# Dense input in the free rows of the pair chunks, five chunks in layer one, eight one-hot tables for all samples

## The reference

```python
e = jnp.stack([tbl_0[ids[:, 0]], ..., tbl_25[ids[:, 25]]], axis=1)      # 512 x 26 x 128
combined = jnp.concatenate([e, r_dense_x[:, None, :]], axis=1)          # 512 x 27 x 128
interact = jnp.einsum('bfd,bgd->bfg', combined, combined)
z = interact[:, _TRIU_I, _TRIU_J]                                       # 512 x 351
h = jnp.concatenate([z, r_dense_x], axis=1)                             # 512 x 479
h = jnp.maximum(h @ W_top1 + b_top1, 0.0)                               # 512
h = jnp.maximum(h @ W_top2 + b_top2, 0.0)                               # 256
y = h @ W_top3                                                          # 1
```

## Time and profile before

| | us |
|---|---|
| median of 3 runs (lowest, highest) | 120.97 (120.47, 121.06) |
| the profiled execution | 120.48 |
| its span | 118.7 |
| PE busy / DVE busy / POOL busy | 110.9 / 93.1 / 71.6 |

### The profile page before, as it was taken

One profiled execution on the slowest core, in us unless ns is written; L12 is line 12 of the kernel. 1 busy time (PEld: TensorE's weight loads), 2 busy tenths in 40 slices (PEclk: granted clock), 3 DMA queues, 4 the chain that ended last, 5 costly groups with the idle time before them and its releaser, 6 DMA issues.

```text
span 118.7 us, 2740 instructions
## 1 busy us (share of the span) xinstructions
PE 110.9 (93%) x794; PEld 88.0 (74%) x794; DVE 93.1 (78%) x379; ACT 50.6 (43%) x147; POOL 71.6 (60%) x80
## 2 busy tenths in 40 slices
PE   4999999999999999999989999799999996999990
PEld 4844454546454799759979898699998895998980
DVE  1699999999999998984999999940689992589312
ACT  5970640506050618930355871105686104586110
POOL 3477777777777776776777777776777750000000
PEclk9999999999999999999999999999999999999999
DMA  3999757454535125897321221221221220000000
GB/s 83 303 319 383 205 168 242 76 215 88 184 111 181 51 68 96 321 355 226 72 51 46 67 45 50 52 63 45 61 59 46 61 50 0 6 0 0 0 0 1
DMA packets 6543, 13.20 MB, mean 111 GB/s; under 512 B 2033, under 2 KB 3569, under 8 KB 6401
## 3 DMA queue, kind: packets, MB, share of 16 engines
q0 software_dynamic: 2336, 4.79, 15.1%
q1 hardware_dynamic: 3328, 5.50, 13.9%
q10 hardware_dynamic: 864, 2.75, 7.5%
HBM read 13.03 MB, written 0.00 MB: 110 GB/s over the span
## 4 chain that ended last, share of the span: by engine, by line
POOL 58%; issue 19%; PE 14%; DMA 5%; POOLq 1%; DVE 1%; ACT 0%; DVEq 0%
POOL rows L329 58%; PE gram_ps L625 6%; PE h_ps L660 3%; DMA idx<-in_ids_dram 3%; DMA rows<-in_tbl_dram,idx 2%; PE turn_ps L645 2%; PE h_ps L645 1%; POOLq L102 1%; PE gram_ps L645 1%; PE turn_ps L631 0%; DVE h L485 0%; DVE h_prod L487 0%; PE turn_ps L598 0%; ACT XT L374 0%; PE gram_ps L631 0%
## 5 line engine op out<-in xcount | busy, mean ns | idle before, releaser
L329 POOL DMA_INDIRECT rows<-in_tbl_dram,idx x73 | 70.5, 966 | 24.0 <-issue 22.0
L430 DVE COPY PAIRS<-gram_ps 27x60 f32<-27x60 f32 (+1 forms) x96 | 24.3, 253 | 11.6 <-PE gram_ps L625 10.2
L625 PE MATMUL gram_ps<-XT 128*123 128x80 f32 x256 | 28.5, 269 | 1.2 <-ACT XT L374 0.9
L625 PEld LDWEIGHTS gram_ps<-XT 128*123 128x123 f32 x256 | 27.9, 188 | 2.0 <-ACT XT L374 1.4
L374 ACT COPY PAIRS<-gram_ps 27x60 f32<-27x60 f32 (+1 forms) x96 | 23.3, 243 | 10.3 <-PE gram_ps L625 9.2
L374 ACT COPY XT<-turn_ps 128x512 f32<-128x512 f32 (+3 forms) x20 | 12.2, 619 | 34.3 <-PE turn_ps L598 18.2
L455 DVE CUSTOM_DVE_ANT_0 few_prod<-rows 128x128 f32<-128x128 f32 x84 | 20.6, 289 | 0.8
L513 DVE TENSOR_SCALAR onehot<-hot_ids,first_row 125x512 bf16<-125x512 int16 (+1 forms) x64 | 19.4, 374 | 2.4 <-DMA hot_ids<-in_hot_ids_dram 2.1
L645 PE MATMUL h_ps<-PAIRS,W1P 128*128 128x128 f32 x130 | 16.8, 276 | 0.2
L645 PEld LDWEIGHTS h_ps<-PAIRS,W1P 128*128 128x128 f32 x130 | 15.5, 192 | 0.5 <-ACT PAIRS L374 0.3
L588 PE MATMUL turn_ps<-onehot,hot_tab 125*128 125x512 bf16 (+3 forms) x56 | 11.7, 351 | 0.0
(11 more groups left out here) (49 smaller groups left out, 87.0 us busy)
## 6 DMA issues: line engine op xcount, KB each, us to landing
hot_tab<-in_hot_dram ACTq DMA_DIRECT2D x5, 512.0 KB, 3.6
rows<-in_tbl_dram SPq DMA_DIRECT2D x128, 0.5 KB
...
rows<-in_tbl_dram,idx POOLq DMA_INDIRECT x73, 2.9
...
```

The source lines that it names most:

```text
L329: pool.indirect_dma_start(rows[:, t, s, :], None, tables[f], bass.IndirectOffsetOnAxis(ap=idx[:, t, f:f + 1], axis=0)) \
L430: return nc.vector.tensor_copy(dst, src)
L625: last = nc.tensor.matmul(gram_ps[0:GRAM_ROWS, 2 * (i % 2) + q // fours, o:o + QUAD * NCOL], four.rearrange("d s f -> d (s f)")[:, 0:GRAM_ ...
```

## The change

- Slots are dealt anew (SLOT_FIELD, with ROW_SLOT from the order of the gathered rows to the slots): the first three gathered fields stand in slots 24 to 26. Rows 24 to 26 are no longer copied from gram's result (KEPT = 24 rows of a quadrant instead of 27; 120 weight columns). The three pairs among them join `few_pairs`: 24 dot products a tile, in goes of 8. With 8 free rows in each quadrant, all 24 fit in chunk 0, so `few` is one transpose and one add.
- The free rows of chunks 1 to 4 (4 quadrants x 8 rows x 4 chunks = 128) hold the dense input, loaded into PAIRS by four DMAs; W1D and its 16 matmuls go, layer one has five chunk matmuls a group. Only chunk 0 is zeroed by ACT.
- Table 25 joins HOT: prepared for all samples, tile 0 of it in the first phase and the rest behind the gram of tile 0 (as table 24 before); table 24 is now done for all samples in the first phase. `late_hot` and the seventh gather group go.
- The first ids load goes from ACT's queue to second place in SP's; the other ids loads are cut 1 + 6 tables instead of 2 + 5; x and its transpose come behind table 2. ACT places the dense input behind its fifth bank.
- The warm-up matmuls use a zeroed tile of their own instead of `ident`, and are 9 instead of 8.

```diff
-FEW = [(a, g) for g in range(FIRST) for a in range(g)]
+KEPT = 24
+APART = NVEC - KEPT
+FEW = [(a, g) for g in range(KEPT, NVEC) for a in range(KEPT, g)] + [(a, g) for g in range(FIRST) for a in range(g)]
...
-SPARE = SLOTS - NVEC
-FEW_PER_CHUNK = 4 * SPARE
-FEW_CHUNKS = -(-len(FEW) // FEW_PER_CHUNK)
-FEW_COLS = (FEW_CHUNKS - 1) * P + SLOTS
+PADDING = SLOTS - NVEC
+SPARE = SLOTS - KEPT
 FEW_PARTS = 3
 FEW_GO = len(FEW) // FEW_PARTS
 ALONE = 3
-assert len(FEW) == FEW_PARTS * FEW_GO and FEW_CHUNKS == 2 and len(FEW) - FEW_PER_CHUNK <= SPARE
-GRAM_ROWS = SLOTS * (QUAD - 1) + NVEC
+assert len(FEW) == FEW_PARTS * FEW_GO <= 4 * SPARE and D == 4 * SPARE * (PART_COLS - 1)
+GRAM_ROWS = SLOTS * (QUAD - 1) + KEPT
...
-WARM_UP = 8
+WARM_UP = 9
 RING = 3
-
-HOT = [1, 5, 7, 9, 12, 18, 24]
+DENSE_AFTER = 4
+
+HOT = [1, 5, 7, 9, 12, 18, 24, 25]
...
 COLD = [f for f in range(NTAB) if f not in HOT]
-GROUP_SIZES = [3, 4, 4, 4, 2, 1, 1]
-LATE_HOT = 25
+GROUP_SIZES = [3, 4, 4, 4, 2, 1]
 ROW_GROUP = 5
 IDS_A_LOAD = 32
 ROWS_FIRST = 64
-LATE_TILE = 2
...
+ROW_FIELD = [NTAB] + COLD
+SLOT_FIELD = [NTAB] + COLD[APART:] + HOT + COLD[:APART]
+ROW_SLOT = [SLOT_FIELD.index(f) for f in ROW_FIELD]
 TURNED = 1 + len(COLD)
 GROUPS = [list(range(1 + sum(GROUP_SIZES[:g]), 1 + sum(GROUP_SIZES[:g + 1]))) for g in range(len(GROUP_SIZES))]
-assert GROUPS[-1] == [TURNED - 1] and GROUPS[ROW_GROUP] == [TURNED - 2]
+assert GROUPS[ROW_GROUP] == [TURNED - 1]
...
-TURNS_AFTER = [[[1], [2, 3], [4, 5], [6]], [[1, 2], [3, 4], [5], []], [[1, 2], [5], [3], [4]]]
-ORDER = [None, range(NG), range(NG - 1), [0] + [g for after in TURNS_AFTER[2] for g in after]]
-EARLY_TURNS = [[], [0], [1], [2, 3], [4, 5], [6]]
...
+TURNS_AFTER = [[[1, 2], [3, 4], [5], []], [[1, 2], [3, 4], [5], []], [[1, 2], [5], [3], [4]]]
+ORDER = [None, range(NG), range(NG), [0] + [g for after in TURNS_AFTER[2] for g in after]]
+EARLY_TURNS = [[], [0], [1], [2, 3], [4], [5], []]
...
             sp.dma_start(idx[:], ids).then_inc(idx_in, 16)
+            sp.dma_start(hot_ids[:, 0, :], hot_ids_in[:, 0, :]).then_inc(ids_first_in, 16)
             for half in range(2):
                 cols = slice(half * HALF_COLS, (half + 1) * HALF_COLS)
                 sp.dma_start(hot_tab[0][:, cols], hot_tables[0].rearrange("(p c) d -> p (c d)", c=CHUNKS)[:, cols]) \
                     .then_inc(hot_half_in if half == 0 else hot_in[0], 16)
-            sp.dma_start(hot_ids[:, 1:3, :], hot_ids_in[:, 1:3, :]).then_inc(ids_next_in, 16)
+            sp.dma_start(hot_ids[:, 1, :], hot_ids_in[:, 1, :]).then_inc(ids_next_in, 16)
             load_hot(sp, 1)
+            sp.dma_start(hot_ids[:, 2:n_hot, :], hot_ids_in[:, 2:n_hot, :]).then_inc(ids_rest_in, 16)
+            load_hot(sp, 2)
             sp.dma_start(rows[:, :, 0, :], x.rearrange("(p t) d -> p t d", t=TILES)).then_inc(dense_in, 16)
-            sp.dma_start(hot_ids[:, 3:n_look, :], hot_ids_in[:, 3:n_look, :]).then_inc(ids_rest_in, 16)
             sp.dma_start(denseT[:], x_t).then_inc(dense_t_in, 16)
-            load_hot(sp, 2)
             fetch_rows(0, ROWS_FIRST)
             sp.dma_start(W1P[:], w1_pairs).then_inc(w1_in, 16)
-            sp.dma_start(W1D[:], w1_dense).then_inc(w1_in, 16)
+            for s in range(4):
+                sp.dma_start(PAIRS[SLOTS * s + KEPT:SLOTS * (s + 1), 1:PART_COLS, :],
+                             x_t.rearrange("(s i k) b -> s i k b", s=4, i=SPARE)[s]).then_inc(dense_pairs_in, 16)
             sp.dma_start(B1[:], b1).then_inc(bias_in, 16)
             sp.dma_start(B2[:], b2).then_inc(w3_in, 16)
             sp.dma_start(W2[:], w2.rearrange("(c p) n -> p c n", p=P)).then_inc(w2_in, 16)
...
-                for g in range(groups_of(t)):
+                for g in range(NG):
                     if t == TILES - 1 and g == ROW_GROUP:
                         continue
                     if t:
 
                         pool.wait_ge(gathered[g], 16 * gather_count(g) * t)
                     for s in GROUPS[g]:
-                        f = SLOT_FIELD[s]
+                        f = ROW_FIELD[s]
                         pool.indirect_dma_start(
                             rows[:, t, s, :], None, tables[f],
                             bass.IndirectOffsetOnAxis(ap=idx[:, t, f:f + 1], axis=0)) \
...
-                    src = banks[32 * j:32 * j + NVEC].rearrange("a k (q n) -> a k q n", q=fours)[:, :, :, cols]
-                    dst = PAIRS[32 * s:32 * s + NVEC, :, b0:b1] \
+                    src = banks[32 * j:32 * j + KEPT].rearrange("a k (q n) -> a k q n", q=fours)[:, :, :, cols]
...
-            def zero_pairs(a, b):
-
-                zeros = few[:, 0:1, 0:P].broadcast_to([P, b - a, P])
-                for c in range(TILES):
-                    cols = slice(c * P, (c + 1) * P)
-                    last = nc.scalar.activation(PAIRS[:, a:b, cols], zeros, ACT.Identity)
-                last.then_inc(pairs_zero, 1)
-
-            act.dma_start(hot_ids[:, 0, :], hot_ids_in[:, 0, :]).then_inc(ids_first_in, 16)
             act.wait_ge(few_cleared, 1)
-            zero_pairs(0, PART_COLS // 2)
-            zero_pairs(PART_COLS // 2, PART_COLS)
-            nc.scalar.activation(XT[:, :, NVEC:SLOTS], few[:, 0:1, 0:SPARE].broadcast_to([P, BATCH, SPARE]),
+            nc.scalar.activation(PAIRS[:, 0, :].rearrange("p (t s) -> p t s", t=TILES),
+                                 few[:, 0:1, 0:P].broadcast_to([P, TILES, P]), ACT.Identity).then_inc(pairs_zero, 1)
+            nc.scalar.activation(XT[:, :, NVEC:SLOTS], few[:, 0:1, 0:PADDING].broadcast_to([P, BATCH, PADDING]),
                                  ACT.Identity).then_inc(padding_clear, 1)
-            act.wait_ge(dense_t_in, 16)
-            copy(XT[:, :, 0], denseT[:]).then_inc(dense_placed, 1)
             for i in range(n_first):
                 empty_bank(act, copy, i)
-                if fills[i][0] == "hot" and RING <= fills[i][1] + RING < n_look:
+                if i == DENSE_AFTER:
+                    act.wait_ge(dense_t_in, 16)
+                    copy(XT[:, :, 0], denseT[:]).then_inc(dense_placed, 1)
+                if fills[i][0] == "hot" and RING <= fills[i][1] + RING < n_hot:
...
+                go = FEW[part * FEW_GO:(part + 1) * FEW_GO]
                 for g in range(NG):
 
-                    if GROUPS[g][0] < FIRST:
+                    if any(ROW_SLOT[r] in pair for r in GROUPS[g] for pair in go):
...
-                nc.vector.tensor_tensor(PAIRS[:, 0, here], PAIRS[:, 0, here], few_bank[t][:, 0:P], ALU.add)
-                nc.vector.tensor_tensor(PAIRS[0:SLOTS, 1, here], PAIRS[0:SLOTS, 1, here],
-                                        few_bank[t][0:SLOTS, P:2 * P], ALU.add).then_inc(turn_read["dve"], 1)
+                nc.vector.tensor_tensor(PAIRS[:, 0, here], PAIRS[:, 0, here], few_bank[t][:, 0:P],
+                                        ALU.add).then_inc(turn_read["dve"], 1)
...
+            nc.vector.memset(warm[:], 0.0).then_inc(warm_ready, 1)
             nc.vector.memset(ident[:], 0.0).then_inc(ident_zero, 1)
...
-                dve.wait_ge([ids_first_in, ids_next_in, ids_next_in, ids_rest_in][min(n, 3)], 16)
+                dve.wait_ge([ids_first_in, ids_next_in, ids_rest_in][min(n, 2)], 16)
...
-                if t == LATE_TILE - 2:
-                    prepare_table(n_hot, slice(LATE_TILE * P, BATCH))
...
+            pe.wait_ge(warm_ready, 1)
+            for _ in range(WARM_UP):
+                nc.tensor.matmul(h2_ps[:, 0:P], warm[:], warm[:], start=True, stop=True)
             pe.wait_ge(ident_ready, 1)
-            for _ in range(WARM_UP):
-                nc.tensor.matmul(h2_ps[:, 0:P], ident[:], ident[:], start=True, stop=True)
...
-                nc.tensor.transpose(few_bank[t][:, 0:P], few[:, t, 0:P], ident[:])
-                nc.tensor.transpose(few_bank[t][0:SLOTS, P:2 * P], few[:, t, P:FEW_COLS], ident[:]).then_inc(turned, 1)
+                nc.tensor.transpose(few_bank[t][:, 0:P], few[:, t, :], ident[:]).then_inc(turned, 1)
...
-            def layer1_dense(t, n):
-                nc.tensor.matmul(h1_out(t, n), W1D[:, n * P:(n + 1) * P], denseT[:, t * P:(t + 1) * P],
-                                 start=True, stop=False)
-
-            def layer1_pairs(t, n):
-
-                order = list(range(FEW_CHUNKS, PART_COLS)) + list(range(FEW_CHUNKS))
+            def layer1(t, n):
+
+                order = [*range(1, PART_COLS), 0]
...
                     last = nc.tensor.matmul(h1_out(t, n), W1P[:, k, n * P:(n + 1) * P], PAIRS[:, k, t * P:(t + 1) * P],
-                                            start=False, stop=(k == order[-1]))
+                                            start=(k == order[0]), stop=(k == order[-1]))
...
-                    pe.wait_ge(w1_in, 32)
+                    pe.wait_ge(w1_in, 16)
+                    pe.wait_ge(dense_pairs_in, 16 * 4)
...
                 for n in range(HC1):
-                    layer1_dense(t, n)
-                    layer1_pairs(t, n)
+                    layer1(t, n)
```

(48 more changed lines are left out.)

32 lines of the change are left out of this document (12 added, 20 removed).

## The result

The changed kernel takes 123.09 us (median of 4 runs, 122.80 to 123.53), the kernel before 121.02 (120.47 to 121.75): a ratio of 1.0211, 95% interval 1.0174 to 1.0249. The forecast was 122.9, slower. The profiled execution took 123.07 us, its span is 121.3. Medians are over all executions of a run, while ratios leave slowed ones out; two of these stand far out, one of 129.25 us in the changed kernel's second run and one of 628.78 us, whose cause is not known, in experiment 7.

The account below looks back on a forecast made before the run. PE looked like the bound at 93% busy, but DVE's chain ahead of gram, with about 0.7 us of slack, was taken to decide; the path's steps end at 120.75, +2.05 us of span, giving 122.9 us, range 121.8 to 124.3.

Parts of the forecast that it names:

- (1): First phase: gram batch 2 waits for pair copies behind 24 products, PE stalls 1.1 us, batch ends at 54.2, +6.0.
- (2): Tile 0: after a `few` transpose and three quarters of table 7, layer one starts at 58.2; first transposes emptied at 60.05.
- (3): Tile 0 to 1: DVE's 5.42 us with two more products puts gram of tile 1 at 65.6, +5.0.
- (4): Tile 1: pair copies, then DVE's chain of 8.58 us, make 18.1 a tile; gram of tile 2 at 83.7, +2.55.
- (5): Tile 2: another 18.1 us, so gram of tile 3 starts at 101.8, +2.4.
- (6): Tail after gram of tile 3: 19.28 us loses 0.12 and one dense matmul, 0.22; end at 120.75.
- The sum: Whole path: span +2.05 us; 122.5 on the profiled execution, 123.0 on the median, 122.9 taken.
- B: Rival, whole kernel: PE's own sum decides because DVE's products hide; 116.3 to 118.1 us; chance 0.09.
- E: Rival: cancellation, DVE's chain shorter by 0.5 a tile and the start gains; 120.5 to 121.7 us; chance 0.07.
- C: Rival, layer one: dense rows land late, each microsecond beyond 9 us from issue delays; 125.5 at 12 us; chance 0.05.
- D: Rival, warm-up: first loads in one queue starve PE, delaying its 2.4 GHz clock; +1 to +2, 124 to 125; chance 0.05.
- what would show the forecast: Signs in the profile: PE below 90%, DVE above 80%, PE gram <- DVE waits about 1.1 us, then 1 or more.

Follow-up runs that it names:

- the changed kernel's second run: The changed kernel itself measured once more, nothing altered, beside other versions on one chip: 123.10 us, ratio 1.0158 to the kernel before.
- experiment 7: Changed kernel with VectorE's bank emptying ahead of more products, first gram batch copied before the third go, dense loads early: 118.46 us, ratio 0.9801.
- Experiment 1: Changed kernel without the three products of slots 24 to 26 (21 a tile, their pairs missing from the output): 120.93 us, ratio 1.0014.
- experiment 5: Changed kernel with VectorE's last emptying of an odd group moved ahead of the third go of products in each tile: 119.72 us, ratio 0.9915.
- experiment 2: Changed kernel with 12 extra matmuls of the removed dense shape, one ahead of each layer-one group in tiles 0 to 2: 123.18 us, ratio 1.0221.

## Why the prediction was right

Read against its steps:

- **(1), first phase: +6.0 forecast, +6.5 measured** (batch 2 ends at 54.74, against 48.22). The mechanism and PE's stall (1.1 forecast, 0.94 measured) are right. The 0.5 missing is the start: a stall of 0 to 0.3 had been booked for ids one place later in the queue. In this execution VectorE got them 0.78 later, PE waited 0.40 us for it in the second table, and VectorE carried the delay through eight tables, so that table 7 started at 39.69, not 39.1. The products took 44.54 to 50.65, 6.11 us for 24 (6.24 forecast).
- **(2), (3): layer one at 58.75 (58.2), gram of tile 1 at 66.19 (65.6).** The distance 7.44 against 7.4 forecast. PE was ready at 65.4 (64.5), so VectorE's emptying decided, as said.
- **(4), (5): 18.15 and 18.11 a tile, forecast 18.1.** Experiment 1 confirms the price of the products (0.67 and 0.43 a tile of 0.75; in tile 2 of that execution VectorE stood idle for 0.44 us ahead of its add), experiment 5 the wait. The weights of gram were forecast to give 0.16 us a tile, and gave about 0.1. The rows to compare are those where PE comes to gram in the same way: straight from its own work, 64 records take 7.02 us with 123 columns (81.15) and 6.92 with 120 (65.08 and 82.21 in experiment 5); after a wait of 0.46 or 0.47 us, 7.11 (99.42) and 7.02 (99.10 in experiment 5). In the changed kernel gram of all three tiles comes after a longer wait, 6.98 or 6.99 us, so that against 81.15 only 0.03 shows. The Trainium skill ("TensorE: Matmul & The Clock Gate", LDWEIGHTS) has the load's time grow with the columns, by its formula 2.5 ns for three. The profile's page agrees on the growth (mean 188 ns a load with 123 columns, 185 with 120), though not on the whole, which by that formula would be 100 to 103 ns. The distance of starts fell by about 1.6 ns a record.
- **(6), tail: 18.85 us against 18.94.**
- **The sum:** +2.05 forecast for the span, +2.6 measured; of the difference 0.5 is the start. Against the medians, which take in several starts, +2.07.

Of the rivals, B (TensorE's sum decides) is refuted by experiment 2 from one side and 1 from the other. E (a cancellation, 120.5 to 121.7) is refuted by the time and by the 18.15 and 18.11 us a tile. C (the dense rows late) did not decide, but was nearer than its 0.05: in one of the six profiles with the loads at their place PE waited for them. D, the first loads in one queue, had its place right and its size too large: 0.5 us later in the median, no loss of clock to be seen. The text on what would show the forecast named about 1.1 us at batch 2 and 1 us or more ahead of each gram: it was 0.94, and 0.79, 0.79, 1.63. It named PE below 90% and DVE above 80%: they stand at 90.2 and 79.7. And the waits ahead of gram are not listed as PE <- DVE, but as "issue". The signs were right in kind, not in each figure.

Where did PE's saving go? By the forecast's sum 2.3 us of work went, and PE's busy time fell by 1.5; with the 2.6 us that the span grew, its idle time is 4.1 us longer. The 1.9 us of old waits, for gathered rows and for ScalarE, gave way to waits that VectorE ended.

That 122.9 came so near to the 123.09 is in part luck. Measured against the profiled execution of the kernel before, which was its fastest, the change cost 0.5 us more than forecast; the median of that kernel lies 0.5 us higher, and so the medians are 2.07 us apart.
